# One order for eight sequences: steps of a two-layer transformer block merged anew, and a block buffer zeroed in eight pieces

## The chip, the cores and the metric

The kernel runs on one core of a Trainium2 chip. The metric is the device time of one execution in microseconds; the time of the kernel before is the median of three runs. The profile shows one execution of its own.

## The reference, cut to what matters

The input is eight sequences of 256 tokens by 128 channels, with a context of 256 by 64 for each. Four blocks follow one another, each added to x:

```python
x = x + _L0_xattn_ref(_layernorm(x), ctx, ...)   # 16 heads of 8: causal self and cross attention, then Wp
x = x + _L0_ffn_ref(_layernorm(x), ...)          # 8 experts, top 2 of a router, F = 512
x = x + _L1_xattn_ref(_layernorm(x), ctx, ctx, ...)  # one head of 128 against the context
x = x + _L1_ffn_ref(_layernorm(x), ...)
# the last one: 16 heads of 64 whose values are mixed per token out of 8 projections
mix_v = jnp.einsum('bthk,bthke->bthe', sigmoid(top2 of gate_v), one_hot)
v = jnp.einsum('bthe,bted->bhtd', mix_v, proj_v)
attn = softmax(q k^T) v
res = jnp.einsum('bthe,bthd,efd->bthf', mask_o, attn, Wo).sum(heads)
```

## The kernel before, in words

All of a sequence's tokens lie on the 128 partitions in two tiles. The work of a sequence is cut into small steps. A step is a name and a number, as ("a_score", 4), and each of the five engines has a function of that name if it has a part in the step. Three groups of steps make a sequence's A side: f (load, first norm, turning, and the eight projections f_stack 0 to 7 into stacked queries and keys), a (first attention: a_max finds row maxima, a_score makes scores and exponentials and, at some numbers, the products with the values; then a_heads, a_project, a_norm2, a_router and a_expert 0 to 7), and c (second attention: c_kv, c_norm, c_norm_apply, c_q, c_max, c_turn, c_out). The last block is the B side: b_norm, b_norm_apply, b_gates (gates, value projections), b_top2 0 to 2 (first maximum, second maximum, sigmoid and product), b_split 0 to 7 (queries and keys as high and low parts), b_max 0 to 7, b_shift, b_score 0 to 7, b_fill, b_mix 0 and 1, b_sel, b_attend 0 to 3, b_weigh, b_gather, b_out.

The A side uses PSUM banks 0 to 3 and the B side banks 4 to 7, so that the B side of a sequence can run within the A side of the next. An order written out by hand sets how. STEPS_A is the list of a sequence's A steps, where the f steps belong to the next sequence. STEPS_B is the list of its B steps, and AFTER_A gives for each of them behind which A step it comes (counted from the start of the same sequence; 56 steps make a sequence, so 65 is in the next one's A side). The last sequence has lists of its own, LAST_B and LAST_AFTER. The function merged() sorts all into one list, and every engine, SyncE's DMA queue too, goes through this one list and issues its own part of each step in that order. There is no other planning: between engines only semaphores order the work.

The mixing is done by matrix products with a block buffer, bd (128 x 2048 fp32). GpSimd zeroes it (line 1151 in b_gates, line 1156 after the second mixing), b_fill copies the mixing weights from DRAM onto its blocks with sixteen DMAs (line 466), b_mix multiplies (line 911), ScalarE copies the result to `at` (line 1106), SyncE stores it to v_d and loads it again, regrouped, as vb (lines 473 and 479), and b_attend multiplies with it (line 928). After the second zeroing b_sel (line 486) puts the output mask there, which b_gather uses (line 942). SyncE also carries f_load, which waits for the sequence's x_a before it loads the next x (line 431), the store and reload of the value projections (lines 443 and 450), and mix_d and sel_d (lines 457 and 458), which wait for the gate product of b_top2 2 (line 1433). The norms are applied by tensor_scalar in line 296, for the second attention in step c_norm_apply.

Of the kernel before, what the change touches and what calls it, by code (L numbers as in the profile page):

```python
# [35 lines left out]
def transformer_program(nc, a, out):  # L36
# [17 lines left out]
    with ctx:  # L54
# [91 lines left out]
        bd = sb("bd", [P, 2048])  # L146
# [17 lines left out]
        def dram(name, shape):  # L164
# [54 lines left out]
            b_mx=16, b_ct=1, b_cc=1, b_st=16, b_ex=16, b_mw=1, b_pd=16, b_pr=32, b_bz=2, b_md=32, b_dm=256, b_do=128,  # L219
# [131 lines left out]
        def run(name, first, end):  # L351
            return [(name, i) for i in range(first, end)]

        STEPS_A = [("a_values", 0), *run("a_max", 0, 7), ("a_shift", 0), ("a_score", 0), ("a_score", 1),
                   ("f_load", 0), *run("a_score", 2, 14), ("a_lastpv", 0), ("a_heads", 0), ("a_project", 0),
                   ("c_kv", 0), ("a_norm2", 0), ("a_norm2_apply", 0), ("a_router", 0), *run("a_expert", 0, 3),
                   ("f_norm", 0), *run("a_expert", 3, 8), ("f_norm_apply", 0), ("a_last", 0), ("c_norm", 0),
                   *run("f_stack", 0, 4), ("c_norm_apply", 0), ("c_q", 0), ("f_stack", 4), ("c_max", 0),
                   ("f_stack", 5), ("f_stack", 6), ("c_turn", 0), ("c_out", 0), ("f_stack", 7)]
        STEPS_B = [("b_norm", 0), ("b_norm_apply", 0), ("b_gates", 0), ("b_top2", 0),  # L360
                   ("b_split", 0), ("b_split", 1), ("b_top2", 1), *run("b_split", 2, 5), ("b_top2", 2),
                   *run("b_split", 5, 8), *run("b_max", 0, 8), ("b_shift", 0), ("b_score", 0), ("b_fill", 0),
                   ("b_mix", 0), ("b_mix", 1), ("b_score", 1), ("b_sel", 0), ("b_score", 2), ("b_score", 3),
                   ("b_attend", 0), ("b_score", 4), ("b_score", 5), ("b_attend", 1),
                   ("b_score", 6), ("b_score", 7), ("b_attend", 2), ("b_attend", 3), ("b_weigh", 0),
                   ("b_gather", 0), ("b_gather", 1), ("b_out", 0)]
        AFTER_A = (65, 69, 70, 71, 71, 72, 75, 75, 76, 77, 78, 79, 79, 81, 85, 86, 86, 90, 91, 91, 92, 92, 93, 96,
# [44 lines left out]
        def sequences(steps):  # L412
# [7 lines left out]
            with nc.Block(no_gpsimd_drain=True) as block:  # L420
# [704 lines left out]
                def _(pool):  # L1125
# [27 lines left out]
                    def b_mix(half):  # L1153
                        if half == 1:
                            pool.wait_ge(S["b_mm"], upto("b_mm", 2 * NT))
                            nc.gpsimd.memset(bd[:, :], 0.0).then_inc(S["b_bz"], 1)
# [336 lines left out]
```

## Time and profile before

| | |
|---|---|
| median of 3 runs | 1322.04 us (1322.01 to 1323.66) |
| profiled execution, its own time | 1322.67 us |
| its span | 1320.9 us |
| TensorE matmul busy | 1137.6 us, 86% |
| VectorE / ScalarE / GpSimd busy | 706.6 (53%) / 494.1 (37%) / 85.0 us (6%) |
| mean granted TensorE clock | 0.847 |

The span is the time from the first to the last instruction. A granted clock of 1.0 is 2.4 GHz and 0.5 is 1.2 GHz. Idle time of an engine is given with what ended it: "[2.10 <-DVE xn_a L296]" is an idle time of 2.10 us, ended by VectorE's instruction of line 296 that writes xn_a. PE is TensorE, DVE VectorE, ACT ScalarE, POOL GpSimd, SPq SyncE's DMA queue.

### The profile page before, as it was taken

How to read it: one execution, taken by the hardware profiler on the slowest of the kernel's cores; microseconds unless marked ns; L12 is line 12 of the kernel's file. 1: busy time of each engine (PE TensorE's matmuls, PEld its weight loads, DVE VectorE, ACT ScalarE, POOL GpSimd, SP SyncE). 2: the span in 40 equal slices, each digit the busy share in tenths (PEclk: the TensorE clock that was granted, in tenths of full speed). 3: DMA queues.
4: the chain of work that ended last, by engine and by line, in shares of the span. 5: the costliest groups of instructions: out<-in, count | busy, mean ns of one | idle time of the engine just before them, and what ended most of it. 6: DMA issues, size and time to landing. Idle time of an engine off the chain costs nothing.

```text
span 1320.9 us, 21222 instructions
## 1 busy us (share of the span) xinstructions
PE 1137.6 (86%) x8499; PEld 883.2 (67%) x8499; DVE 706.6 (53%) x1867; ACT 494.1 (37%) x1022; POOL 85.0 (6%) x134
## 2 busy tenths in 40 slices
PE   6888779989989988989988988988998998985696
PEld 4547545777668765877577855976577766874475
DVE  5514466646565557547665658546664656423500
ACT  4233415352534425451634334442535253422120
POOL 0010002000110002000200011000200011000000
PEclk8558959899789979998889978998889978977556
DMA  7000000242020420142022221042023210133222
GB/s 212 0 1 4 3 0 1 48 69 65 8 49 17 69 55 21 29 76 57 6 49 47 47 47 46 5 77 63 1 48 67 64 40 13 29 56 84 52 44 52
DMA packets 198032, 56.85 MB, mean 43 GB/s; under 512 B 173568, under 2 KB 193838, under 8 KB 197934
## 3 DMA queue, kind: packets, MB, share of 16 engines
q1 hardware_dynamic: 195630, 51.20, 19.9%
q10 hardware_dynamic: 2304, 4.29, 1.1%
q8 instruction: 67, 1.10, 0.3%
q14 instruction: 31, 0.25, 0.1%
HBM read 31.36 MB, written 24.12 MB: 42 GB/s over the span
## 4 chain that ended last, share of the span: by engine, by line
PE 75%; DVE 11%; ACT 7%; issue 3%; SPq 3%; DMA 2%; ACTq 0%; DVEq 0%
PE bank L928 10%; PE bank L737 10%; PE bank L773 9%; PE bank L884 5%; PE bank L663 5%; PE bank L843 4%; PE bank L624 3%; PE bank L678 3%; PE bank L588 3%; DVE negmax L1261 3%; ACT pa L1022 3%; PE bank L942 2%; PE bank L860 2%; PE bank L688 2%; PE bank L911 2%
## 5 line engine op out<-in xcount | busy, mean ns | idle before, releaser
L1022 ACT ACTIVATE pa<-bank 128x512 f32<-128x512 f32 x224 | 123.4, 596 | 122.8 <-PE bank L678 75.8
L1261 DVE TENSOR_REDUCE negmax<-bank 128x2 f32<-128x512 f32 (+1 forms) x224 | 139.0, 683 | 41.9 <-PE bank L526 22.1
L1039 ACT ACTIVATE pa<-bank,b_c 128x256 f32<-128x256 f32 x256 | 107.5, 471 | 128.6 <-PE bank L737 127.3
L928 PE MATMUL bank<-vb,pb 128*128 128x65 f32 x1024 | 137.1, 299 | 4.2 <-issue 4.2
L928 PEld LDWEIGHTS bank<-vb,pb 128*128 128x128 f32 x1024 | 132.8, 214 | 10.3 <-issue 7.9
L737 PE MATMUL bank<-xnT_a,w 128*128 128x256 f32 x512 | 138.1, 417 | 0.1
L773 PE MATMUL bank<-w,pa 128*128 128x128 f32 x1024 | 124.2, 276 | 0.0
L773 PEld LDWEIGHTS bank<-w,pa 128*128 128x128 f32 x1024 | 121.9, 192 | 3.2
L1101 ACT ACTIVATE pb<-bank 128x512 f32<-128x512 f32 x128 | 69.9, 602 | 125.4 <-PE bank L888 125.4
L737 PEld LDWEIGHTS bank<-xnT_a,w 128*128 128x128 f32 x512 | 101.1, 208 | 17.3 <-ACT pa L1039 0.5
L1415 DVE TENSOR_REDUCE negc<-bank 128x2 f32<-128x512 f32 x128 | 80.0, 684 | 58.8 <-PE bank L860 58.6
L1166 POOL TENSOR_SCALAR_AFFINE_SELECT pa<-pa 128x256 f32<-128x256 f32 (+1 forms) x96 | 53.8, 568 | 666.6 <-ACT pa L1022 665.4
L663 PE MATMUL bank<-pa,va 128*32 128x256 f32 (+1 forms) x1024 | 72.1, 412 | 6.6 <-issue 4.8
L1008 ACT ACTIVATE hi_part<-bank,lo_bias,lo_c 128x256 fp32r<-128x256 f32 x128 | 63.2, 568 | 32.5 <-PE bank L588 32.5
L843 PE MATMUL bank<-xnT_b,wqk_t 128*128 128x256 f32 x256 | 71.0, 409 | 4.5 <-DVE qk_lo L1407 4.5
L1111 ACT COPY pvs<-bank 128x512 f32<-128x512 f32 x16 | 16.8, 1049 | 151.1 <-PE bank L942 151.1
L624 PE MATMUL bank<-ks,qs 32*128 32x256 f32 x384 | 57.8, 407 | 13.8 <-DVE negmax L1261 10.7
L1251 DVE SCALAR_TENSOR_TENSOR qs<-bank,bias_c,hi_part 128x256 fp32r<-128x256 f32 x64 | 27.7, 480 | 77.1 <-ACT hi_part L1008 77.1
L678 PE MATMUL bank<-qs,ks 32*128 32x256 f32 x256 | 52.7, 392 | 18.1 <-ACT pa L1022 15.1
L588 PE MATMUL bank<-xnT_f,w_stack 128*128 128x256 f32 x192 | 56.0, 432 | 12.5 <-DVE qs L1251 9.6
L884 PE MATMUL bank<-qk_hi,qk_lo 64*128 64x256 f32 x256 | 55.5, 360 | 9.1 <-ACT pb L1101 7.8
L1346 DVE SCALAR_TENSOR_TENSOR x_a<-bank,wr,x_a 128x128 f32<-128x128 f32 x128 | 38.7, 343 | 44.4 <-PE bank L773 44.1
(240 smaller groups left out, 1706.3 us busy)
## 6 DMA issues: line engine op xcount, KB each, us to landing
v_d<-at SPq DMA_DIRECT2D x32, 256.0 KB, 3.3
vb<-v_d SPq DMA_DIRECT2D x32, 256.0 KB, 6.0
at_d<-at SPq DMA_DIRECT2D x32, 256.0 KB, 2.1
at<-at_d SPq DMA_DIRECT2D x32, 256.0 KB, 4.4
pv_d<-pvs SPq DMA_DIRECT2D x8, 512.0 KB, 3.1
pvs<-pv_d SPq DMA_DIRECT2D x16, 256.0 KB, 4.2
w<-in_L_ffn_W_dram ACTq DMA_DIRECT2D x1, 2048.0 KB, 11.5
bd<-mix_d SPq DMA_DIRECT2D x128, 8.0 KB
```

What stands on the lines that cost most here:

```text
L588: mm = pe.matmul(BA[2 + u % 2][:, c * T:(c + 1) * T], w_stack[0:rows, kind, g, :], rhs[:, :], start=True, stop=True)
L624: mm = pe.matmul(BA[j][:, c * T:(c + 1) * T], qs[strips[j], sc, g, qt * P:(qt + 1) * P], ks[strips[j], sc, g, :], start=(c == 0), stop=Tru ...
L663: mm = pe.matmul(dst, va[:, sc, kt, h * DV:h * DV + 32], rhs, start=(kt == 0), stop=(sc == SELF or kt == 1), skip_group_check=True)
L678: mm = pe.matmul(BA[i][:, kt * T:(kt + 1) * T], ks[strips[i], CROSS, k, kt * P:(kt + 1) * P], qs[strips[i], CROSS, k, :], start=True, stop ...
L737: mm = pe.matmul(BA[u % 2][:, c * T:(c + 1) * T], w1[:, e, f:f + P], xnT_a[:, :], start=True, stop=True)
L773: mm = pe.matmul(BA[2 + e % 2][:, t * P:(t + 1) * P], hT[:, (2 * e + f // 2) % 4, f % 2, t * P:(t + 1) * P], w2[:, e, f, :], start=(f == 0 ...
L843: mm = pe.matmul(BB[(u + 2) % 4][:, c * T:(c + 1) * T], wqk_t[:, u // 4, 2 * (u % 4) + c, :], xnT_b[:, :], start=True, stop=True)
L884: pe.matmul(BB[i][:, kt * T:(kt + 1) * T], kq[halves[i], 1, pr, keys], qq[halves[i], 0, pr, :], start=(kt == 0 and part == 0), stop=(part ...
L928: mm = pe.matmul(BB[2 + qt][:, i * (DH + 1):(i + 1) * (DH + 1)], pb[:, h % NPB, kt * T + qt * P:kt * T + (qt + 1) * P], vb[:, kt, h, :], s ...
L1022: nc.scalar.activation(pa[:, e % NPA, :], BA[e % 2][:, :], ACT.Exp, scale=SC0).then_inc(S["a_ex"], 1)
L1039: ins = nc.scalar.activation(hT[:, u % 4, c, :], BA[u % 2][:, c * T:(c + 1) * T], ACT.Relu, bias=b1_c[:, k:k + 1])
L1261: nc.vector.tensor_reduce(negmax[:, i:i + ng], BA[j][:, :].rearrange("p (g k) -> p g k", g=ng), AX, ALU.max, negate=True).then_inc(S["a_mx ...
```

## The change

Both lists of B steps, the list of A steps and their positions are written anew, and the memset of the block buffer is cut into eight of 256 columns each, with the semaphore counts that go with it. In the steady order the part around the second attention goes from "b_score 0, b_fill, b_mix 0, a_last, c_norm, f_stack 0 to 3, b_mix 1, c_norm_apply, b_score 1, c_q, f_stack 4, b_sel, c_max, b_score 2, f_stack 5 and 6, c_turn, b_score 3, b_attend 0, b_score 4, c_out, f_stack 7" to "b_fill, (f_norm_apply,) b_mix 0, a_last, c_norm, f_stack 0, b_score 0, b_mix 1, c_norm_apply, b_score 1, f_stack 1, c_q, f_stack 2, c_max, f_stack 3, b_sel, f_stack 4, c_turn, b_score 2, f_stack 5, c_out, f_stack 6, b_score 3, f_stack 7, b_attend 0, b_score 4".

```diff
-            b_mx=16, b_ct=1, b_cc=1, b_st=16, b_ex=16, b_mw=1, b_pd=16, b_pr=32, b_bz=2, b_md=32, b_dm=256, b_do=128,
+            b_mx=16, b_ct=1, b_cc=1, b_st=16, b_ex=16, b_mw=1, b_pd=16, b_pr=32, b_bz=16, b_md=32, b_dm=256, b_do=128,
...
-        STEPS_A = [("a_values", 0), *run("a_max", 0, 7), ("a_shift", 0), ("a_score", 0), ("a_score", 1),
-                   ("f_load", 0), *run("a_score", 2, 14), ("a_lastpv", 0), ("a_heads", 0), ("a_project", 0),
-                   ("c_kv", 0), ("a_norm2", 0), ("a_norm2_apply", 0), ("a_router", 0), *run("a_expert", 0, 3),
-                   ("f_norm", 0), *run("a_expert", 3, 8), ("f_norm_apply", 0), ("a_last", 0), ("c_norm", 0),
-                   *run("f_stack", 0, 4), ("c_norm_apply", 0), ("c_q", 0), ("f_stack", 4), ("c_max", 0),
-                   ("f_stack", 5), ("f_stack", 6), ("c_turn", 0), ("c_out", 0), ("f_stack", 7)]
-        STEPS_B = [("b_norm", 0), ("b_norm_apply", 0), ("b_gates", 0), ("b_top2", 0),
-                   ("b_split", 0), ("b_split", 1), ("b_top2", 1), *run("b_split", 2, 5), ("b_top2", 2),
-                   *run("b_split", 5, 8), *run("b_max", 0, 8), ("b_shift", 0), ("b_score", 0), ("b_fill", 0),
-                   ("b_mix", 0), ("b_mix", 1), ("b_score", 1), ("b_sel", 0), ("b_score", 2), ("b_score", 3),
-                   ("b_attend", 0), ("b_score", 4), ("b_score", 5), ("b_attend", 1),
-                   ("b_score", 6), ("b_score", 7), ("b_attend", 2), ("b_attend", 3), ("b_weigh", 0),
-                   ("b_gather", 0), ("b_gather", 1), ("b_out", 0)]
-        AFTER_A = (65, 69, 70, 71, 71, 72, 75, 75, 76, 77, 78, 79, 79, 81, 85, 86, 86, 90, 91, 91, 92, 92, 93, 96,
-                   96, 96, 102, 103, 105, 106, 109, 109, 109, 112, 113, 114, 114, 115, 116, 116, 119, 119, 120)
+        STEPS_A = [("a_values", 0), *run("a_max", 0, 7), ("a_shift", 0), *run("a_score", 0, 14), ("a_lastpv", 0),
+                   ("a_heads", 0), ("a_project", 0), ("a_norm2", 0), ("c_kv", 0), ("a_norm2_apply", 0),
+                   ("a_router", 0), ("a_expert", 0), ("a_expert", 1), ("f_load", 0), *run("a_expert", 2, 6),
+                   ("f_norm", 0), ("a_expert", 6), ("a_expert", 7), ("f_norm_apply", 0), ("a_last", 0),
+                   ("c_norm", 0), ("f_stack", 0), ("c_norm_apply", 0), ("f_stack", 1), ("c_q", 0), ("f_stack", 2),
+                   ("c_max", 0), ("f_stack", 3), ("f_stack", 4), ("c_turn", 0), ("f_stack", 5), ("c_out", 0),
+                   ("f_stack", 6), ("f_stack", 7)]
+        STEPS_B = [("b_norm", 0), ("b_norm_apply", 0), ("b_gates", 0), ("b_top2", 0), *run("b_split", 0, 8),
+                   *run("b_max", 0, 4), ("b_top2", 1), *run("b_max", 4, 8), ("b_top2", 2), ("b_shift", 0),
+                   ("b_fill", 0), ("b_mix", 0), ("b_score", 0), ("b_mix", 1), ("b_score", 1), ("b_sel", 0),
+                   ("b_score", 2), ("b_score", 3), ("b_attend", 0), ("b_score", 4), ("b_score", 5),
+                   ("b_attend", 1), ("b_score", 6), ("b_score", 7), ("b_attend", 2), ("b_attend", 3),
+                   ("b_weigh", 0), ("b_gather", 0), ("b_gather", 1), ("b_out", 0)]
+        AFTER_A = (67, 67, 68, 68, 70, 71, 74, 75, 76, 77, 78, 78, 79, 80, 84, 84, 85, 88, 88, 89, 89, 90, 93, 95,
+                   96, 99, 99, 100, 105, 107, 110, 111, 111, 112, 113, 114, 114, 115, 116, 116, 119, 119, 120)
...
-        LAST_B = [("b_norm", 0), ("b_norm_apply", 0), ("b_gates", 0), ("b_top2", 0), ("b_split", 0), ("b_top2", 1),
-                   *run("b_split", 1, 5), ("b_top2", 2), *run("b_split", 5, 8), ("b_max", 0), ("b_fill", 0),
-                   *run("b_max", 1, 4), ("b_mix", 0), ("b_sel", 0), ("b_mix", 1), *run("b_max", 4, 8),
+        LAST_B = [("b_norm", 0), ("b_norm_apply", 0), ("b_gates", 0), ("b_top2", 0), *run("b_split", 0, 3),
+                   ("b_top2", 1), ("b_top2", 2), *run("b_split", 3, 8), ("b_max", 0), ("b_fill", 0),
+                   *run("b_max", 1, 4), ("b_sel", 0), ("b_mix", 0), ("b_mix", 1), *run("b_max", 4, 8),
                    ("b_shift", 0), *run("b_score", 0, 4), ("b_attend", 0), ("b_score", 4), ("b_score", 5),
                    ("b_attend", 1), ("b_score", 6), ("b_score", 7), ("b_attend", 2), ("b_attend", 3),
-                   ("b_gather", 0), ("b_weigh", 0), ("b_gather", 1), ("b_out", 0)]
...
+                   ("b_gather", 0), ("b_gather", 1), ("b_weigh", 0), ("b_out", 0)]
...
                     def b_fill(_):
                         sp.wait_ge(S["b_md"], upto("b_md", 32))
-                        sp.wait_ge(S["b_bz"], upto("b_bz", 1))
+                        sp.wait_ge(S["b_bz"], upto("b_bz", 8))
...
                     def b_sel(_):
-                        sp.wait_ge(S["b_bz"], upto("b_bz", 2))
+                        sp.wait_ge(S["b_bz"], upto("b_bz", 16))
...
+                    def clear_blocks():
+                        for i in range(8):
+                            nc.gpsimd.memset(bd[:, 256 * i:256 * i + 256], 0.0).then_inc(S["b_bz"], 1)
+
                     def b_gates(_):
...
-                        nc.gpsimd.memset(bd[:, :], 0.0).then_inc(S["b_bz"], 1)
+                        clear_blocks()
 
                     def b_mix(half):
                         if half == 1:
                             pool.wait_ge(S["b_mm"], upto("b_mm", 2 * NT))
-                            nc.gpsimd.memset(bd[:, :], 0.0).then_inc(S["b_bz"], 1)
+                            clear_blocks()
```

## Rows read from the trace of the kernel before

**Rows 1.** The page: busy us, share and instructions of each engine; clock in tenths.

```profile
PE 1137.6 (86%) x8499; PEld 883.2 (67%) x8499; DVE 706.6 (53%) x1867; ACT 494.1 (37%) x1022; POOL 85.0 (6%) x134
PEclk8558959899789979998889978998889978977556
```

**Rows 2.** Stretches: length, busy us of each engine, granted clock, DMA share, GB/s.

```profile
559.81:705.78 145.97, 132.24 (x1058) 103.07 (x1057) 87.83 (x230) 60.64 (x126) 10.43 (x14) 0.91 0.22 43
...
576.00:582.00 6.00, 5.92 (x34) 4.58 (x36) 0.22 (x2) 2.96 (x6) 0.00 (x0) 0.72 1.17 190
...
628.00:642.00 14.00, 12.09 (x52) 6.48 (x48) 4.52 (x20) 6.39 (x12) 2.56 (x3) 0.63 0.05 14
...
563.00:593.00 30.00, 26.66 (x227) 21.88 (x226) 13.84 (x42) 17.05 (x37) 1.80 (x1) 0.94 0.51 84
```

**Rows 3.** Timeline of TensorE, second attention: start, length, instruction, idle before it.

```profile
570.05 1.99 PE L588 MATMUL bank<-xnT_f,w_stack 128*128 128x256 f32 x8 [1.24 <-DVE qs L1251]
...
576.08 0.44 PE L520 MATMUL bank<-ident,xn_a 128*128 128x128 f32 x2 [2.10 <-DVE xn_a L296]
```

**Rows 4.** Timeline of VectorE and GpSimd at the same place.

```profile
573.98 2.05 DVE L296 TENSOR_SCALAR xn_a<-x_a,mv_a,rstd_a 128x128 f32<-128x128 f32 x2
...
574.08 1.80 POOL L1156 MEMSET bd<- 128x2048 f32 x1 [58.09 <-PE bank L911]
```

**Rows 5.** Line 296: ns min/median/max, first and last start.

```profile
L296 DVE TENSOR_SCALAR xn_a<-x_a,mv_a,rstd_a x32: 339/346/1982, 106.1 to 1149.9; 128x128 f32<-128x128 f32 x32
```

**Rows 6.** Timeline of TensorE: score 3 of the first attention, and the second norm.

```profile
632.71 1.28 PE L678 MATMUL bank<-qs,ks 32*128 32x256 f32 x4 [0.48 <-ACT pa L1022]
...
672.45 0.69 PE L520 MATMUL bank<-ident,xn_a 128*128 128x128 f32 x2 [2.66 <-DVE xn_a L296]
```

**Rows 7.** Waits of TensorE in 559 to 705 us: total, times, longest; score 13.

```profile
PE bank L697 <- ACT pa L1022: 0.9, 2, 0.8
```

**Rows 8.** Line 1138: a memset of 256 columns on GpSimd, ns.

```profile
L1138 POOL MEMSET negc<- x1: 311/311/311, 2.6 to 2.6; 128x256 f32 x1
```

**Rows 9.** Timeline of VectorE, then of TensorE: top-2, reductions, products of experts.

```profile
650.62 0.68 DVE L312 TENSOR_REDUCE top_bm<-at 128x64 f32<-128x512 f32 x1
...
679.22 2.48 DVE L1415 TENSOR_REDUCE negc<-bank 128x2 f32<-128x512 f32 x4 [0.35 <-PE bank L860]
...
688.14 1.95 PE L773 MATMUL bank<-w,pa 128*128 128x128 f32 x16
...
705.71 3.84 PE L773 MATMUL bank<-w,pa 128*128 128x128 f32 x32
```

**Rows 10.** Timeline, last sequence: gate product, fills of the block buffer, first mixing.

```profile
1226.04 0.60 DVE L1433 TENSOR_TENSOR gates<-eg,top_b 128x256 f32<-128x256 f32 x1
...
1229.02 5.77 SPq L466 DMA_DIRECT2D bd<-mix_d  x16
...
1236.09 3.68 PE L911 MATMUL bank<-pvs,bd 64*128 64x64 f32 x32 [3.05 <-DMA bd<-mix_d]
```

**Rows 11.** Timeline of SyncE's queue in a steady period: mixing weights, fills.

```profile
674.12 0.66 SPq L457 DMA_DIRECT2D mix_d<-gates  x1
...
678.57 6.78 SPq L466 DMA_DIRECT2D bd<-mix_d  x16
```

**Rows 12.** Timeline of TensorE, first sequence, second attention.

```profile
149.25 0.44 PE L520 MATMUL bank<-ident,xn_a 128*128 128x128 f32 x2 [2.58 <-DVE xn_a L296]
```

**Rows 13.** Timeline of TensorE, last A window: mix 1, attend 0, C's output.

```profile
1150.40 2.00 PE L911 MATMUL bank<-pvs,bd 64*128 64x64 f32 x32 [1.14 <-ACT at L1106]
...
1164.60 7.06 PE L928 MATMUL bank<-vb,pb 128*128 128x65 f32 x32 [4.00 <-issue]
...
1173.60 2.07 PE L814 MATMUL bank<-pa 128*128 128x128 f32 x8
```

**Rows 14.** Timeline, last sequence: last value loads issued, attend 0.

```profile
1251.75 6.04 SPq L479 DMA_DIRECT2D vb<-v_d  x4
...
1264.11 7.09 PE L928 MATMUL bank<-vb,pb 128*128 128x65 f32 x32
```

More of the change, by code:

```diff
@@ L374, in transformer_program @@
                    ("b_shift", 0), *run("b_score", 0, 4), ("b_attend", 0), ("b_score", 4), ("b_score", 5),
                    ("b_attend", 1), ("b_score", 6), ("b_score", 7), ("b_attend", 2), ("b_attend", 3),
-                   ("b_gather", 0), ("b_weigh", 0), ("b_gather", 1), ("b_out", 0)]
-        LAST_AFTER = (57, 66, 75, 76, 76, 76, 76, 76, 76, 76, 76, 89, 104, 109, 109, 109, 109, 109, 110, 110, 110,
-                   110, 117, 117, 117, 117, 117, 117, 117, 117, 117, 117, 118, 126, 129, 136, 136, 143, 147, 149,
-                   149, 154, 154)
+                   ("b_gather", 0), ("b_gather", 1), ("b_weigh", 0), ("b_out", 0)]
@@ L380, in transformer_program @@
+        LAST_AFTER = (62, 66, 67, 70, 70, 73, 81, 86, 90, 90, 90, 90, 90, 90, 90, 90, 90, 90, 95, 111, 111, 112,
+                   113, 119, 121, 125, 129, 130, 130, 130, 130, 130, 130, 130, 130, 130, 135, 135, 135, 135, 135,
+                   135, 140)
         assert len(LAST_AFTER) == len(LAST_B)
```

## The prediction, made before the changed kernel ran

> **What bounds the kernel now.** I read the page's busy shares and its row of granted clock first. TensorE is busy for 86% of the span and no other engine for more than 53%, at a mean clock of 0.85 [rows 1]. So TensorE is the bound, and two things can be won: its idle time and the stretches in which it runs at half clock (1.2 instead of 2.4 GHz). Next come stretches of one steady period (sequence q on the A side, q-1 then q on the B side; 146 us). In it TensorE is busy for 132.2 of 146.0 us, at 0.91 [rows 2]. So a period holds 13.7 us of idle and 26 us at half clock (2 x 0.09 x 146), which cost 13 us more. Last I read TensorE's timeline through that period for where the idle lies, and those of VectorE and SyncE for what ends it.
>
> Three places hold most of it. (1) Around the start of the C attention TensorE waits 1.24 us for VectorE's splits, then 2.10 us for the normalised x [rows 3]. The second wait is not arithmetic: the pair of tensor_scalars took 2.05 us, and the 1.80 us clearing of the block buffer on GpSimd started 0.1 us after it [rows 4]; the median of one such operation is 0.346 us, so a free pair takes some 0.6 to 0.7 [rows 5]. Behind the two waits the clock is 0.72 for 6 us, 3.4 us at half, a loss of 1.7 us [rows 2]. (2) In the score stage single waits for ScalarE's exponentials of 0.5 to 0.8 us [rows 6, 7], with the clock at 0.63 over 14 us [rows 2]. (3) The second norm, 2.66 us waited for VectorE [rows 6].
>
> **The change, part by part.** Arithmetic and bytes are the same except for the clearing: one memset of 2048 columns becomes eight of 256. All the rest is order on each engine, also on SyncE's queue.
>
> *Region C of a steady period (six times, q = 1 to 6).* Before: score 0, mix 0, f_stack 0 to 3, mix 1, the normalised x, score 1. After: mix 0, f_stack 0, score 0, mix 1, normalised x, score 1, then f_stack 1 to 7 one by one between the steps of C. VectorE now has two splits instead of eight ahead of the normalised x, so it applies the norm while TensorE is at score 0 and mix 1: both waits have cover, and the clearing, which waits for mix 1, starts after the tensor_scalars. That returns 1.24 + 2.10 = 3.34 us [rows 3], and with no idle ahead of it the half-clock stretch should go, 1.7 us [rows 2]. Late next is ScalarE's order: the exponentials of C stand behind f_stack 2, and the turn of the probabilities waits for them. I put that at 0.7 us and other small ones at 0.6 (nearest rows: the waits of 0.48 [rows 6] and 1.24 [rows 3]); bounds 0 and 3.34, all of it coming back. Gain 3.34 + 1.7 - 1.3 = 3.7 us, times six: 22.4 us (bounds 10 and 30).
>
> *The clearing in pieces.* A piece of 256 columns took 0.31 us [rows 8], so eight take 1.80 to 2.5 us. At the start of a sequence's B side nobody waits; there its step also moves ahead of the masking of the fifth score step, but its wait has been met for long by then. If my order is off by a microsecond and a norm meets the clearing again, the rows give only the two ends: let in after one piece, 0.31 us [rows 8], or held through all eight, 1.8 us and more [rows 4]. Taken at nothing, with up to 1.9 us a period inside the bounds above.
> What bears on it is the Trainium skill, "SBUF — State Buffer", section "Who interferes with whom": VectorE in a two-port mode and GpSimd exclude each other for a whole instruction, whoever started first. By it the 2.05 us is that lock, pieces bring a meeting down to one piece, and the gain of region C stands even with the order slightly off; without it an unlucky meeting costs six times 1.7 us, 10 us of the sum.
>
> *The mixing and its feeders (SyncE, VectorE).* The second half of the top-2 (six operations of 512 columns, each like the first of [rows 9], 0.72 us apart, 4.3 us) and the gate product leave the score stage and go among the experts, the first ahead of the first accumulation, the second behind the third. f_load moves from early in the score stage to behind expert 1, so SyncE's queue no longer waits there for the projected x with the store and reload of the projected values behind it; these go out earlier. Nobody on TensorE waited for them: 0. The product, though, now comes late. From its end to the first mixing product the last sequence took 9.4 us (1226.64 to 1236.09) [rows 10]; in the period the stores and sixteen fills alone took 11.2 us [rows 11], some 12.5 with the landing (1.3 us in rows 10). Time available: expert 2's products end at 690.1, those of expert 7 at 709.5 [rows 9]; two B maxima steps fewer (by net count) lie between, and the tokens' turn is added, so 18.4 us. The product needs of that the reductions of two B maxima steps (2.48 us, behind 0.9 us of products), one accumulation of 0.6 and its own 2.7: 6.7. That leaves 11.7 us against 9.4 to 12.5: wait 0 to 0.8 us, taken at 0.3, inside the 0.6 above. Expert waits: VectorE has the router (twenty small operations, an estimated 0.2 us each) behind four reductions (2.5) and then the 4.3 us before the first accumulation, which comes at about 685 by this; it is needed by expert 2's products, which before started at 688.1 [rows 9]. Three us of cover, nothing charged.
>
> *Score stage and second norm (seven times).* B's norm and gates move one score step earlier or ahead: its turn fills the 0.48 us before score 3 [rows 6], and a split's products fill the 0.95 us (0.78 + 0.17) before score 13 [rows 7]. B maxima 0 and 1 go among the heads. Their reductions (four, 2.5 us) lie under TensorE's turns but push the heads' arithmetic by about 0.5 us, while the products fill what was waited. The 2.66 us before the router stays [rows 6]: its cover, the keys of C, is the same. Net 1.3 us, seven times: 9.1 us. Bounds: -0.4 us each (the reductions in full on the chain: 0.9 late against 0.5 filled) and +3.3 (half of the 5.2 us lost to half clock over 628 to 642 returns too).
>
> *First sequence without a B side.* Same interleave, and no mixing. 2.58 us were waited for the normalised x [rows 12], and the f_stacks that stood before it now fill the C chain. Gain 3 us (1 to 5).
>
> *Last A window.* The wait before mix 1 goes (1.14 us); B's attend 0 waited 4.00 us for values sent off behind mix 1 [rows 13]. These go 1.1 us earlier, and C's output products, 2.07 us at half clock and about 1.2 at full, move from behind it into its wait [rows 13]. Gain 3 us (1 to 5), counting 0.7 of clock.
>
> *Last sequence alone.* The gate product comes before splits 3 to 7 rather than before 5 to 7, some 1.0 us earlier; mix 0 waited for its fills [rows 10]. Against it, SyncE now stores the first mixed half behind the second clearing: two stores more ahead of the last loads, which were issued until 1257.8, while attend 0 began at 1264.1 [rows 14] with hardly any slack. Taken at +0.5 (-1 to +1.5). Exchanging b_weigh and b_gather 1 changes no engine's own order.
>
> Sum: 22.4 + 9.1 + 3 + 3 + 0.5 = 38 us. The profiled execution took 1322.7 us (span 1320.9), so 1284.7; the median of the runs lies 0.6 us below it: 1284.
>
> **Rivals.**
> - *Idle that only moves* (chance 0.25). ScalarE is busy for 17 of 30 us in region C [rows 2], in strict order, so f_stack's two activations may make C wait where it did not. For: TensorE waited for ScalarE at many places already [rows 6, 7]. Against: single waits there are under 1 us. Then region C gives 10 to 12 (no clock won), the score stage 4, the ends 4: 20 us, 1302.
> - *Clock comes back in the score stage too* (0.12). The half-clock stretch behind the B gathers ends once TensorE has been busy without a break; the gates' products now follow earlier. Two us more a sequence, 14 us: 1270. Against: the stretch before it (the A maxima, bound by VectorE's reductions) is unchanged.
> - *The fill comes late: slower* (0.07). The mixing waits for the fill, and everything on TensorE queues behind it. It outweighs the gain of 38 us over seven sequences from 5.4 us each, that is a stall of 3.7 plus 1.7 of clock: the way from product to last fill would have to take over 15.4 us, where rows show 9.4 to 12.5 [rows 10, 11]. At 17 us: 1330.
> - *No change* (0.04). The clearing still blocks a norm and the new order only exchanges waits: 1321.
>
> **How the numbers follow.** My forecast has 0.52, with a range of its own of 1276 to 1294. The range for 8 in 10 takes in the first rival and half of the second: 1267 to 1306. A measurement of this kernel tells 0.2% (2.6 us) from no change. Faster by more: 0.52 + 0.25 + 0.12 and a little of the rest, 0.90; within: 0.03; slower: 0.07.
>
> **What would show it.** Right: the tensor_scalar pair of C's norm at 0.6 us in every period; TensorE over 28 us or more of 30 busy in region C with its clock at 1.00; a period of about 141 us; half-clock time at the second norm unchanged. Wrong: waits of TensorE on the fills before mix 0 above 1 us; waits of the turn of C's probabilities above 1.5 us; an accumulation later than its expert's products. If the periods shrink by under 2 us each, the first rival holds.

## The result and the profile after

| | before | after |
|---|---|---|
| median | 1322.03 us (1318.88 to 1323.66) | 1278.06 us (1274.52 to 1278.99) |
| ratio, 95% interval | | 0.9666 (0.9645 to 0.9687) |
| profiled execution, its span | 1322.67, 1320.9 us | 1274.52, 1272.8 us |
| mean granted clock | 0.847 | 0.855 |

The kernel became 44 us faster, where 38 were forecast (1284, range 1267 to 1306). The page of the kernel after, to be read against [rows 1]: TensorE has 18.7 us less to do (the same 8499 products, more of them at full clock) in a span 48 us shorter.

```profile
PE 1118.9 (88%) x8499; PEld 874.8 (69%) x8499; DVE 700.1 (55%) x1867; ACT 491.0 (39%) x1022; POOL 82.8 (7%) x246
PEclk8557958899889979898889978998889988998556
```

The last products of expert 7 mark each sequence. In the chain that ended last (start, length, work) they stand like this after the change:

```profile
136.09 3.77 PE bank L773 x32
265.17 3.77 PE bank L773 x32
403.47 3.77 PE bank L773 x32
543.36 3.77 PE bank L773 x32
683.30 3.77 PE bank L773 x32
...
1103.14 3.77 PE bank L773 x32
```

From the second period on it is now 139.9 us each (the first is 138.3), where [rows 2] have one of 146.0; the kernel before alternated between 144.2 and some 146. Between the second and the last marker the kernel before took 1142.61 - 269.12 = 873.5 us, the one after 838.0: 35.5 us in six periods. Another 4.0 come ahead of the second marker, and 8.6 behind the last one (178.3 to 169.7 us). That makes 48.1 us between the two profiled spans; the medians give 44, since the profiled run of after was its fastest.

Windows of the kernel after (length, busy us of each engine, clock): the period of [rows 2], region C, the stretch behind the second norm, and the last A window.

```profile
543.36:683.30 139.94, 130.02 (x1057) 102.65 (x1057) 86.74 (x230) 60.13 (x126) 9.98 (x28) 0.91 0.23 45
547.00:577.00 30.00, 29.21 (x269) 24.51 (x266) 14.85 (x46) 19.45 (x42) 2.09 (x8) 1.00 0.52 84
650.00:660.00 10.00, 9.64 (x37) 7.91 (x38) 7.81 (x28) 3.66 (x10) 0.00 (x0) 0.58 0.00 0
...
1120.00:1140.00 20.00, 17.66 (x155) 15.46 (x154) 3.04 (x10) 6.51 (x12) 0.00 (x0) 0.93 0.35 51
```

TensorE's timeline of the same period (start, length, idle before): the two waits that remain in region C, then those of the heads and the second norm.

```profile
557.48 1.13 PE L799 MATMUL bank<-pa 128*128 128x256 f32 x4 [0.18 <-ACT pa L1067]
560.98 0.66 PE L806 MATMUL bank<-ident,pa 128*128 128x128 f32 x4 [0.52 <-ACT pa L1072]
...
645.01 0.44 PE L520 MATMUL bank<-ident,xn_a 128*128 128x128 f32 x2 [1.26 <-DVE xn_a L1306]
...
650.36 0.69 PE L520 MATMUL bank<-ident,xn_a 128*128 128x128 f32 x2 [2.67 <-DVE xn_a L296]
```

The reader is to see that the waits of [rows 3] are gone, that region C is busy for 29.21 of 30 us at full clock (26.66 at 0.94 before, [rows 2]), and that the second norm kept its wait (2.66 us in [rows 6]). Its half clock did not stay the same, it grew. Twelve us around that norm, before and then after, have a clock of 0.72 and 0.57, which is 6.7 and 10.3 us at half:

```profile
671.00:683.00 12.00, 10.55 (x51) 8.46 (x52) 8.12 (x31) 3.95 (x10) 0.00 (x0) 0.72 0.54 111
```

```profile
647.00:659.00 12.00, 9.33 (x35) 7.43 (x34) 9.43 (x41) 3.50 (x10) 0.00 (x0) 0.57 0.04 12
```

In the score stage it is the other way round. Fourteen us there, after the change, are at 0.76 in each of three periods; before it was 0.63 [rows 2] in the periods of some 146 us and 0.76 in those of 144.2:

```profile
606.00:620.00 14.00, 12.47 (x77) 7.35 (x73) 8.91 (x27) 6.81 (x14) 0.29 (x1) 0.76 0.05 17
```

Line 296, now never held up (against [rows 5]), and the clearing in pieces:

```profile
L296 DVE TENSOR_SCALAR xn_a<-x_a,mv_a,rstd_a x32: 337/343/348, 105.6 to 1110.4; 128x128 f32<-128x128 f32 x32
```

```profile
L1148 POOL MEMSET bd<- x128: 308/312/315, 92.8 to 1197.9; 128x256 f32 x128
```

The fill of the block buffer, which the prediction put at the edge, and the first mixing behind it, which did not wait (SyncE's queue, then TensorE):

```profile
675.20 0.37 SPq L457 DMA_DIRECT2D mix_d<-gates  x1
...
677.55 6.66 SPq L466 DMA_DIRECT2D bd<-mix_d  x16
```

```profile
687.43 2.00 PE L911 MATMUL bank<-pvs,bd 64*128 64x64 f32 x32
```

### The profile page after: what moved, and what is told of

Read it like the earlier page. It is cut to its first block, busy times and chain, and to the rows that moved or that the text cites. A ratio compares the mean times of both kernels' runs of the same rounds, so it can differ in the third digit from the quotient of the medians.

```text
span 1272.8 us, 21333 instructions
## 1 busy us (share of the span) xinstructions
PE 1118.9 (88%) x8499; PEld 874.8 (69%) x8499; DVE 700.1 (55%) x1867; ACT 491.0 (39%) x1022; POOL 82.8 (7%) x246
## 4 chain that ended last, share of the span: by engine, by line
PE 74%; DVE 12%; ACT 7%; issue 2%; SPq 2%; DMA 2%; ACTq 0%; DVEq 0%
PE bank L737 10%; PE bank L928 10%; PE bank L773 9%; PE bank L843 5%; PE bank L884 5%; PE bank L663 4%; PE bank L624 3%; PE bank L678 3%; DVE negmax L1265 3%; PE bank L911 3%; ACT pa L1022 2%; PE bank L588 2%; PE bank L942 2%; ACT hi_part L1008 2%; PE bank L832 2%
## 5 line engine op out<-in xcount | busy, mean ns | idle before, releaser
L737 PE MATMUL bank<-xnT_a,w 128*128 128x256 f32 x512 | 141.8, 429 | 0.1
L928 PEld LDWEIGHTS bank<-vb,pb 128*128 128x128 f32 x1024 | 129.6, 209 | 7.8 <-ACT pb L1101 3.0
L928 PE MATMUL bank<-vb,pb 128*128 128x65 f32 x1024 | 133.8, 294 | 1.2 <-ACT pb L1101 0.8
L737 PEld LDWEIGHTS bank<-xnT_a,w 128*128 128x128 f32 x512 | 107.0, 219 | 18.4 <-ACT pa L1039 0.7
L1148 POOL MEMSET bd<- 128x256 f32 x128 | 33.4, 312 | 745.2 <-PE bank L911 414.3
L1411 DVE TENSOR_TENSOR qk_lo<-bank,qk_hi 128x512 fp32r<-128x512 f32 x64 | 43.8, 690 | 65.9 <-ACT qk_hi L1093 65.9
L1111 ACT COPY pvs<-bank 128x512 f32<-128x512 f32 x16 | 16.9, 1058 | 150.3 <-PE bank L942 150.2
L1170 POOL TENSOR_SCALAR_AFFINE_SELECT pa<-pa 128x256 f32<-128x256 f32 (+1 forms) x96 | 46.7, 495 | 369.5 <-ACT pa L1022 368.3
L663 PE MATMUL bank<-pa,va 128*32 128x256 f32 (+1 forms) x1024 | 66.1, 385 | 4.4 <-issue 2.5
L884 PE MATMUL bank<-qk_hi,qk_lo 64*128 64x256 f32 x256 | 57.1, 356 | 9.9 <-ACT pb L1101 8.5
L678 PE MATMUL bank<-qs,ks 32*128 32x256 f32 x256 | 52.3, 393 | 14.8 <-ACT pa L1022 11.7
L843 PEld LDWEIGHTS bank<-xnT_b,wqk_t 128*128 128x128 f32 x256 | 44.9, 191 | 23.4 <-DVE qk_lo L1411 13.1
## 6 DMA issues: line engine op xcount, KB each, us to landing
w<-in_L_ffn_W_dram ACTq DMA_DIRECT2D x1, 2048.0 KB, 10.5
```

Source lines behind the costliest of these rows:

```text
L663: mm = pe.matmul(dst, va[:, sc, kt, h * DV:h * DV + 32], rhs, start=(kt == 0), stop=(sc == SELF or kt == 1), skip_group_check=True)
L678: mm = pe.matmul(BA[i][:, kt * T:(kt + 1) * T], ks[strips[i], CROSS, k, kt * P:(kt + 1) * P], qs[strips[i], CROSS, k, :], start=True, stop ...
L737: mm = pe.matmul(BA[u % 2][:, c * T:(c + 1) * T], w1[:, e, f:f + P], xnT_a[:, :], start=True, stop=True)
L843: mm = pe.matmul(BB[(u + 2) % 4][:, c * T:(c + 1) * T], wqk_t[:, u // 4, 2 * (u % 4) + c, :], xnT_b[:, :], start=True, stop=True)
L884: pe.matmul(BB[i][:, kt * T:(kt + 1) * T], kq[halves[i], 1, pr, keys], qq[halves[i], 0, pr, :], start=(kt == 0 and part == 0), stop=(part ...
L928: mm = pe.matmul(BB[2 + qt][:, i * (DH + 1):(i + 1) * (DH + 1)], pb[:, h % NPB, kt * T + qt * P:kt * T + (qt + 1) * P], vb[:, kt, h, :], s ...
```

## The experiments

The median of the kernel before in the same group of runs is given with the first of each group. Four groups: the first four below, the next four, then e4, e12 and e11, and last e14.

**1. The new order with one whole clearing (e1).**

```diff
-                        for i in range(8):
-                            nc.gpsimd.memset(bd[:, 256 * i:256 * i + 256], 0.0).then_inc(S["b_bz"], 1)
+                        for i in range(1):
+                            nc.gpsimd.memset(bd[:, :], 0.0).then_inc(S["b_bz"], 8)
```

> The changed kernel with the block buffer zeroed in one memset of 2048 columns again; the new order stays. Theory (the order is what counts, since the norm of C is now applied before the clearing starts): no change within 2 us of the changed kernel, about 1278 us, and the tensor_scalar pair of C's norm stays at 0.6 to 0.7 us. Rival (the pieces count): the pair or another VectorE operation meets the 1.80 us clearing in each of six periods and the time rises by 6 to 10 us, to 1285 to 1288.

Measured: 1277.75 us (before 1320.10), ratio 0.9681 (0.9654 to 0.9707). With the new order the pieces bring nothing: the clearing no longer meets a norm (line 296 is 348 ns at the longest).

**2. The old order with the clearing in pieces (e2).** The diff's `clear_blocks`, `b_bz=16` and the two waits, without the lists.

> The kernel before with nothing changed but the clearing in eight pieces. Theory A (one VectorE instruction is let in after one piece): the pair of tensor_scalars falls from 2.05 us to 0.9 to 1.2, TensorE's wait before C's turn from 2.10 to about 1.1, some 6 us over six periods and up to 10 more if the half-clock stretch behind it goes: 1306 to 1316 us. Theory B (the pieces follow one another so closely that VectorE is held through all eight, 2.1 us): 1322 to 1324 us.

Measured: 1405.27 us, ratio 1.0679 (1.0601 to 1.0757), and a miss for both theories. The four runs spread from 1388.25 to 1418.56 us, more than those of any other kernel here, so it is 68 to 98 us slower (85 by the median); the profile is of the fastest. Line 296 in this kernel, then TensorE's timeline, SyncE's queue and the window behind:

```profile
L296 DVE TENSOR_SCALAR xn_a<-x_a,mv_a,rstd_a x32: 336/343/492, 104.5 to 1219.5; 128x128 f32<-128x128 f32 x32
```

```profile
598.87 0.44 PE L520 MATMUL bank<-ident,xn_a 128*128 128x128 f32 x2 [0.65 <-DVE xn_a L296]
...
610.51 5.99 PE L928 MATMUL bank<-vb,pb 128*128 128x65 f32 x32 [2.40 <-ACT pb L1101]
```

```profile
599.89 5.74 SPq L479 DMA_DIRECT2D vb<-v_d  x4
```

```profile
611.00:669.00 58.00, 57.07 (x343) 47.71 (x342) 24.11 (x50) 6.99 (x12) 0.00 (x0) 0.51 0.17 38
```

The pieces did their work: the longest tensor_scalar fell from 1982 ns [rows 5] to 492, and the norm's wait from 2.10 us [rows 3] to 0.65. But the mixed values, which SyncE stores and loads again, came no earlier behind mix 1. From mix 1's first product TensorE now needed 11.9 us to be ready for attend 0 and not 14.5 (1.45 of it from the norm's wait, the rest from products that ran at full clock), and it waited there for 2.40. The wait is put down to ScalarE's exponentials, which is the last event the profile shows; that it is the reload is suggested by the distance from the reload's first issue to attend 0, and shown by experiment 5. It is 610.51 - 599.89 = 10.6 us here, with a wait. In the kernel before, these two stood like this:

```profile
575.65 5.94 SPq L479 DMA_DIRECT2D vb<-v_d  x4
```

```profile
586.51 3.79 PE L928 MATMUL bank<-vb,pb 128*128 128x65 f32 x32
```

10.9 us, no wait. Over e2's six periods the distance with a wait is 10.5 to 11.4 us, and the kernel before has one period with a wait of 0.19 us at 11.2: it had a few tenths of a microsecond to spare at this place, at most. Behind the 2.40 us TensorE ran at half clock for 58 us although busy for 57.1 of them. From marker to marker the periods alternate between 164.4 and 149.6 us; in the shorter ones, with waits of 2.3 to 3.2 us, the clock is back after some 10 us. Why the same wait costs so differently stays open.

**3. The new kernel with region C in its old order (e3).** The A list, the places of b_score 0, b_fill, b_mix and the positions of region C as before; score stage, top-2, gates and pieces as after.

> The changed kernel with the second attention's region in its old order (f_stack 0 to 3 together, score 0 ahead of mix 0, mix 1 behind f_stack 3, C's output behind attend 0 and score 4); experts, score stage, last sequence and the pieces stay new. Theory (most of the gain is region C, with its half-clock stretch, and the last A window): the time rises by 22 to 32 us, to 1300 to 1310. Rival (score stage and tail made most of it): it rises by less than 12, to 1290 at most.

Measured: 1338.39 us, ratio 1.0135 (1.0105 to 1.0165): not 10 to 20 us of gain but 18 of loss. It has the pieces and the old order of region C like e2. Its trace is of the longest of the four runs (1359.65 us; the others took 1336.77 to 1339.16), so it tells where the kernel waits, and not how the 18 us divide. Attend 0 waits in each of the six periods, for 2.3 to 3.1 us, for instance

```profile
593.41 6.85 PE L927 MATMUL bank<-vb,pb 128*128 128x65 f32 x31 [2.56 <-ACT pb L1100]
```

at 10.8 us behind the first issue of its reload. So e2's wait is in this kernel too; that it makes up the 18 us isn't shown.

**4. The kernel before with region C alone in its new order (e5).** The inverse, with the whole clearing:

```diff
-                   *run("f_stack", 0, 4), ("c_norm_apply", 0), ("c_q", 0), ("f_stack", 4), ("c_max", 0),
-                   ("f_stack", 5), ("f_stack", 6), ("c_turn", 0), ("c_out", 0), ("f_stack", 7)]
+                   ("f_stack", 0), ("c_norm_apply", 0), ("f_stack", 1), ("c_q", 0), ("f_stack", 2),
+                   ("c_max", 0), ("f_stack", 3), ("f_stack", 4), ("c_turn", 0), ("f_stack", 5), ("c_out", 0),
+                   ("f_stack", 6), ("f_stack", 7)]
...
-                   *run("b_split", 5, 8), *run("b_max", 0, 8), ("b_shift", 0), ("b_score", 0), ("b_fill", 0),
-                   ("b_mix", 0), ("b_mix", 1), ("b_score", 1), ("b_sel", 0), ("b_score", 2), ("b_score", 3),
+                   *run("b_split", 5, 8), *run("b_max", 0, 8), ("b_shift", 0), ("b_fill", 0), ("b_mix", 0),
+                   ("b_score", 0), ("b_mix", 1), ("b_score", 1), ("b_sel", 0), ("b_score", 2), ("b_score", 3),
```

> The complement: the kernel before with nothing new but region C's order (mix 0, f_stack 0, score 0, mix 1, C's norm, the other f_stacks one by one, C's output ahead of attend 0). The clearing is one memset. Theory: six periods give 3.5 to 4 us each, the first sequence 3, the last A window 5 to 6: 30 us, about 1292. Rival (the parts only work together): at most 15 us, 1307 or more.

Measured: 1291.11 us, ratio 0.9782 (0.9757 to 0.9807): 29.0 us of gain, as the theory had it (30). The prediction's terms that lie in this part are region C, first sequence and last A window: 22.4 + 3 + 3 = 28.4 us. The parts don't add up, though: region C alone gives -29, everything else alone +18 (e3), both together -44.

**5. The pieces in the old order, mix 1 earlier (e9).** e2 with mix 1 and its store behind f_stack 0 instead of f_stack 3: the position 102 becomes 99.

> The kernel before with the clearing in eight pieces and, of the new order, only one move: mix 1 behind f_stack 0 instead of behind f_stack 3. Theory (with the pieces alone TensorE reached attend 0 before the regrouped values had landed, waited 2.4 us and more there, and then ran at half clock for 8 to 45 us; mix 1 some 3 to 4 us earlier takes that away): 1295 to 1312 us, faster than the kernel before, and no wait of attend 0 on the values above 1 us in the steady periods. Rival (the pieces themselves upset something else, on GpSimd or VectorE): it stays above 1370.

Measured: 1330.65 us (before 1324.26), ratio 1.0057 (1.0037 to 1.0076). Its timeline of TensorE:

```profile
580.34 0.44 PE L520 MATMUL bank<-ident,xn_a 128*128 128x128 f32 x2 [2.54 <-DVE xn_a L296]
...
590.77 3.79 PE L928 MATMUL bank<-vb,pb 128*128 128x65 f32 x32
```

One number in a list takes nearly all of e2's loss away, and in the steady periods attend 0 no longer waits: the wait for the regrouped values, with the half clock behind it, is e2's cause. The forecast of 1295 to 1312 was still missed. Without f_stack 1 to 3 ahead of mix 1 the clearing is early, yet the norm waits 2.54 us again while line 296 itself takes 348 ns at most. So that wait belongs to the order too, not only to the clearing. VectorE has all the splits of f_stack 0 to 3 ahead of the norm, and the last of them waits for ScalarE:

```profile
578.89 0.88 DVE L1255 SCALAR_TENSOR_TENSOR ks<-bank,bias_c,hi_part 128x256 fp32r<-128x256 f32 x2 [1.37 <-ACT hi_part L1008]
579.68 0.60 DVE L296 TENSOR_SCALAR xn_a<-x_a,mv_a,rstd_a 128x128 f32<-128x128 f32 x2
```

**6. The new kernel with the mixing later (e10).** Mix 1 moves from behind f_stack 0 to behind c_max, and so behind score 1, f_stack 1 and f_stack 2 (position 99 to 104); score 1 keeps its place. Of the edit:

```diff
-                    ("b_fill", 0), ("b_mix", 0), ("b_score", 0), ("b_mix", 1), ("b_score", 1), ("b_sel", 0),
+                    ("b_fill", 0), ("b_mix", 0), ("b_score", 0), ("b_score", 1), ("b_mix", 1), ("b_sel", 0),
```

> The changed kernel with mix 1 moved back, behind score 1 and f_stack 2 (7 to 8 us later), so that its store and reload end some 4 to 5 us after TensorE reaches attend 0. Theory: a wait of 4 to 5 us before attend 0 in each of six periods and a half-clock stretch behind each: 30 us of waits and 20 to 90 us of clock, 1325 to 1400 us. Rival (f_stacks one by one and the norm's place are the gain, the mixing's lead is not needed): at most 12 us over the changed kernel, 1290.

Measured: 1363.10 us, ratio 1.0304 (1.0285 to 1.0324): the place of mix 1 alone decides between 44 us of gain and 39 of loss. All waits of line 928 in this kernel (total, times, longest):

```profile
PE bank L928 <- issue: 35.0, 8, 8.1
```

Its period is 150.2 us, 10.3 longer than after. In the one read (from 565.8), 4.5 of that are this wait and 1.5 a wait for C's norm, for which mix 1 had been cover; TensorE is busy for 134.8 us instead of 130.0 with the same 1057 products, which is clock.

**7. The gate product behind expert 5 instead of expert 3 (e6).** One position, 90 to 92.

> The changed kernel with the gate product (b_top2 2) behind expert 5's accumulation instead of expert 3's, about 7 us later. In the changed kernel the last fill was issued at 684.2 and mix 0 began at 687.4, so some 2 us of slack. Theory: mix 0 waits about 5 us for its fills in each of seven periods, 35 us, and the clock may fall to half behind each wait, 10 to 60 us more: 1315 to 1370 us. Rival (there is much more slack than I think, or the DMAs go faster without neighbours): under 1290.

Measured: 1304.78 us, ratio 0.9855 (0.983 to 0.9881), 27 us slower than after. The first mixing now waits for its fills:

```profile
PE bank L911 <- DMA bd<-mix_d: 18.7, 7, 3.6
```

That is 2.7 us on average, not the 5 of the theory, and the time lies between its 1315 and the rival's 1290. The prediction's rival "fill late" is a real mechanism. Two experts later makes a wait of up to 3.6 us; the kernel after, with the product where the change puts it, has no such wait.

**8. The last sequence kept busy (e8).** Products on constants that nobody reads, in the last sequence alone (22 before split 7; more before maxima, scores and mixing):

```diff
+                    def warm(n):
+                        if now[0] == B - 1:
+                            for _ in range(n):
+                                pe.matmul(BA[3][:, 0:T], w1[:, 0, 0:P], w1[:, 0, 0:T], start=True, stop=True)
```

> The changed kernel with extra products of constants on TensorE (128x256, into a free bank, read by nobody) ahead of its waits in the last sequence: 22 before split 7, 5, 3 and 2 around the maxima, 6 and 4 before the two mixings, 6 before the shift, 2 before each score that waits. In the changed kernel the last 85 us ran at half clock though TensorE was 93% busy in most of them. Theory (the clock stays low because of the short idle times; filling them brings it back): the tail's products take half the time, 15 to 28 us less, 1250 to 1263. Rival (the extra products only take time): 1278 to 1290.

Measured: 1266.65 us, ratio 0.9572 (0.9552 to 0.9592), 11 us faster than after; the theory had 1250 to 1263. In the kernel after, then in this one, the last stretches are

```profile
1180.00:1205.00 25.00, 14.75 (x107) 12.01 (x108) 10.87 (x18) 2.73 (x5) 2.09 (x8) 0.50 0.20 25
1205.00:1272.80 67.80, 52.00 (x332) 46.13 (x330) 5.34 (x18) 10.75 (x18) 0.00 (x0) 0.55 0.28 59
```

```profile
1180.00:1205.00 25.00, 25.00 (x174) 19.84 (x173) 10.22 (x17) 2.74 (x5) 2.09 (x8) 1.00 0.13 11
1205.00:1263.00 58.00, 43.28 (x371) 37.55 (x369) 6.13 (x20) 10.76 (x18) 0.00 (x0) 0.82 0.36 76
```

**9. C's output products late in the last A window (e4).** Behind score 4 of sequence 6, as before the change, in this window only.

```diff
+            order.remove(("c_out", 0, B - 1))
+            order.insert(order.index(("b_score", 4, B - 2)) + 1, ("c_out", 0, B - 1))
```

> The changed kernel with one step moved back in the last A window only: C's output (c_out of sequence 7) behind attend 0 and score 4 of sequence 6, as in the kernel before. Theory (c_out's products shorten the wait before attend 0, and a longer wait there brings half clock behind it, which made the last window give 6.7 us instead of the 3 I had forecast): 3 to 7 us slower than the changed kernel, 1281 to 1285 us, with a wait of 2 to 3 us before attend 0 and half clock behind it. Rival (the earlier mixing alone did it): within 1.5 us.

Measured: 1284.63 us (before 1323.26), ratio 0.9715 (0.9685 to 0.9746), against 0.9666 for after: 6.5 us, as the theory had it, but not by the wait of 2 to 3 us that it expected. Attend 0 waited 0.94 us; the price is in the clock:

```profile
1120.00:1140.00 20.00, 16.54 (x95) 14.38 (x96) 2.92 (x9) 4.86 (x11) 0.00 (x0) 0.58 0.57 72
```

The kernel after has 0.93 there. In both the clock falls ahead of attend 0, behind waits of 0.89 and 1.84 us in C's chain. With C's output of 2.07 us in the gap before attend 0 it came back within 3.4 us, without it after 17.

**10. Five constant products before the second norm's turn (e12).** `warm(5, BA[0])` in a_norm2_apply, every sequence.

> The changed kernel with five extra products of constants (128x256, into a bank free at that point, read by nobody) in the 2.67 us that TensorE waits for the second norm, in all eight sequences. Behind that wait the clock was 0.58 over 10 us, 8.4 us at half. Theory: the half-clock stretch goes, up to 4 us a sequence, 15 to 32 us in all: 1246 to 1263 us. Rival (other waits around it, 1.26 and 0.46 us, keep the clock low all the same): 1275 to 1281.

Measured: 1287.61 us, ratio 0.9743 (0.9708 to 0.9777): 9.5 us slower than after, a miss. Its windows: the norm's stretch, and a later one.

```profile
650.00:660.00 10.00, 8.25 (x53) 6.71 (x52) 8.25 (x31) 3.72 (x10) 0.00 (x0) 1.00 0.00 1
578.00:603.00 25.00, 24.74 (x150) 19.73 (x152) 13.82 (x27) 0.14 (x1) 0.00 (x0) 0.50 0.29 64
```

Behind the norm the clock is full where it was 0.58, and most periods took 138 us. But in one (145.3 us) a stretch at half clock, with TensorE busy for 24.7 of 25 us, came up among B's scores, though the gap ahead of it (0.69 us) is the same as in the others. And the part behind the last marker is 18 us longer, more than the periods had won. Of it 17 lie in the last A window, and there a gap did change:

```profile
1117.85 5.03 PE L938 MATMUL bank<-vb,pb 128*128 128x65 f32 x32 [2.45 <-issue]
```

```profile
1120.00:1171.00 51.00, 40.59 (x263) 37.23 (x262) 7.10 (x31) 6.42 (x10) 2.08 (x8) 0.50 0.18 42
```

With full clock ahead of it TensorE was ready for attend 0 12.1 us after mix 1's first product, and 13.6 in the kernel after; the values were no earlier, so it waited 2.45 us instead of 0.75, and the next 51 us ran at half clock. It is e2's sequence of events again: time won ahead of attend 0 is waited for there.

**11. All gaps filled (e11).** The norm's five, one product before scores 1 and 2 and before the waits of maxima 5 and 6, about half of e8's fillers in the last sequence, and there b_sel behind mix 1 instead of ahead of mix 0.

```diff
+                     def warm(n, bank, width=T):
+                         for _ in range(n):
+                             pe.matmul(bank[:, 0:width], w_stack[:, Q0, 0, :], w_stack[:, Q0, 0:width // P, :],
+                                       start=True, stop=True)
...
+                                if m >= 5 and c == 0 and now[0] > 0:
+                                    warm(1, BB[0], P)
...
+                                    if n in (1, 2) and kt == 0 and i == 0:
+                                        warm(1, BA[3])
...
+                        warm(5, BA[0])
```

> As the kernel with the norm's gap filled, and besides one product more before scores 1 and 2, one of 128 columns before each wait of the last two rounds of the first attention's maxima, and the waits of the last sequence filled with fewer products than in the earlier trial (12 before split 7 instead of 22, 1 to 3 elsewhere instead of 2 to 6), its b_sel behind mix 1. Theory: 4 us a sequence at the norm, 2 to 5 at maxima and scores, and 15 to 20 in the last sequence: 1205 to 1240 us. Rival (the extra products delay what they stand before as much as the clock gives back): 1262 or more.

Measured: 1239.40 us, ratio 0.9395 (0.9339 to 0.945): 6% faster than before and 39 us faster than the changed kernel, with 300 products more. What b_sel's move gives of that wasn't measured alone. Its page, and four of its markers:

```profile
PE 1133.6 (91%) x8799; PEld 884.9 (71%) x8799; DVE 699.2 (56%) x1867; ACT 489.0 (39%) x1022; POOL 83.0 (7%) x246
PEclk8559857999899998999899999999899999965997
```

```profile
404.04 3.77 PE bank L787 x32
540.80 3.77 PE bank L787 x32
677.52 3.77 PE bank L787 x32
814.44 3.77 PE bank L787 x32
```

**12. The same without the norm's filler (e14).**

```diff
-                        warm(5, BA[0])
```

> The kernel with every gap filled (1239.4 us), without its five constant products ahead of the second norm's turn; the fillers before scores 1 and 2, before the waits of A maxima 5 and 6 and in the last sequence stay. Their result is read by nobody. Theory: the norm's filler alone only moved the half clock to the scores (1287.6 us against 1278.1), so it is worth nothing without the others but something with them: the norm's wait of 2.67 us and the half clock behind it come back in each of seven periods, about 2 to 3 us each, and the kernel takes 1255 to 1262 us, with a period of 139 us. Rival: the norm's filler costs as much as it gives here too (its products hold up what stands behind them), the gain of the filled kernel comes from the fillers before the scores and maxima, and this kernel takes 1230 to 1240 us.

Measured: 1253.22 us (before 1324.49), ratio 0.9475 (0.9447 to 0.9503); periods of 137.2 to 139.9 us; the theory had 1255 to 1262. So the norm's filler is worth 14 us by the medians and 11 by the ratios beside the others (e11's slowest run, 1251.73 us, lies among e14's), and costs 9.5 without them. Fillers can't be priced one by one here.

## Why the prediction was right, step by step

- *Region C* (22.4 us, with first sequence and last window 28.4): right in place and mechanism. Both waits of [rows 3] went; late next was ScalarE, as said, with 0.18 and 0.52 us where 1.3 were allowed. Idle returned 3.34 - 0.70 = 2.6 us; the clock went from 0.94 to 1.00 over 30 us, 1.8 us (1.7 forecast). 4.4 us a period instead of 3.7; from the marker to the first wait among the next sequence's maxima the traces have 54.7 and 50.4 us. Alone it gave 29 us (e5).
- *Idle that only moves*: this rival fell, since the periods shrank by 5.9 us on average, not under 2. In the old order such a move did happen (e2), to attend 0 and not, as the rival had it, to ScalarE.
- *Clearing in pieces at nothing*: right for the new order (e1). The step held it to be an insurance worth up to 1.9 us a period. In the old order it costs 68 to 98 us (e2). The Trainium skill ("SBUF — State Buffer", "Who interferes with whom") has the lock for a whole instruction; the trace agrees: 1982 ns beside a whole clearing, 492 beside pieces, a delay of 149 ns, under the 312 of one piece. That was right and still decided nothing, since a second wait stood right behind the first.
- *What the prediction did not see*: the lead of the mixing. It named attend 0's wait only for the last window. In the steady period attend 0 was covered by a few tenths of a microsecond, so any waiting taken away between mix 1 and attend 0 had to come back there. The new order gave both at once: mix 1 moved ahead of f_stack 1 to 3, so f_stack 1 to 7 and C's output stand between it and attend 0, where f_stack 4 to 6 stood, and 16.1 us pass from one to the other instead of 14.5. e10 shows that the gain hangs on this. The working had no term for it, so that no loss came from it was luck.
- *Mixing and feeders*: nobody waited, as charged (0.3 us were allowed). The fills' issues end at 684.2, with the landing of 1.3 us [rows 10] at 685.5, so 1.9 us are to spare, where the working had -0.8 to 2.3 (11.7 against 12.5 and 9.4); e6 confirms the rival's mechanism at a distance of two experts.
- *Score stage and second norm* (1.3 us a sequence): 5.9 - 4.4 = 1.5 a period on average, which is right in the waits and lucky in the size. The waits of [rows 7] and the 0.48 of [rows 6] are gone, the wait at the heads grew from 0.83 to 1.26 us (the push by VectorE's reductions, put at 0.5), and the norm's is unchanged, all as forecast. The clock is not. The prediction had the half-clock time at the second norm unchanged, and it grew by 3.6 us in the period read, a loss of 1.8. Where the period before was some 146 us the score stage gave that much back (0.63 to 0.76 over 14 us: 3.6 us less at half), and where it was 144.2 it had nothing to give. So against the short periods the whole change is worth 4.3 us, region C's part alone, and against the long ones 6 us and more. *Clock comes back in the score stage too* therefore came true in the long periods only and was lost again at the norm: the period's mean clock stays at 0.91. Why the norm's half-clock stretch grew isn't shown.
- *First sequence*: 3 + 1.3 forecast ahead of the second marker, 4.0 measured.
- *The mis-sized term* is the last A window, 3 us. From the marker to attend 1 it returned 6.5 us (34.9 to 28.4): attend 0 waited 0.75 instead of 4.00 us and took 3.76 instead of 7.06 [rows 13]. I had counted 0.7 us of clock; e4 gives 6.5 for C's output in the gap alone.
- *Last sequence alone*: 0.5 forecast, 8.6 - 6.5 = 2.1 us measured. Of these, 1.8 come ahead of the last B norm, mostly from the output products of sequence 6 at full clock instead of half (line 953: 2.06 us instead of 3.57). Another 0.75 come up to mix 0: its wait of 3.05 us for the fills [rows 10] became one of 1.69 for a reduction, while the wait before split 7 grew from 3.81 to 5.81. Against these, 0.44 are lost up to attend 0, which now waits 0.40.

Sum of what was measured between the two profiled spans: 4.0 + 35.5 + 8.6 against 4.3 + 30 + 3.5.

## What to carry to other kernels

Before a wait is taken away, measure how far its successors are from waiting: the distance from a transfer's issue to its first reader, in a place where it waits and in one where it doesn't, bounds the slack (here 10.9 without a wait against 10.5 to 11.4 with one). A gain upstream is kept only when the slowest chain downstream (here mix, store, reload, attend) starts earlier by as much. And price a gap by what the clock does behind it: in e2 gaps of much the same length stood in periods of 149.6 and of 164.4 us. A filler must be judged on the whole run.

## What the runs showed of the hardware that was not expected

- Half clock can stay although TensorE is busy. In e2 it was busy for 57.1 of 58 us at a granted clock of 0.51, and in e12 for 24.7 of 25 at 0.50. In both kernels other periods with the same order ran at full clock in the same place. What decides between the two isn't settled.
- The same four stores of the mixed values occupied SyncE's queue for 8.07 us in the kernel before, 4.92 after and 12.09 in e10, because ScalarE's copies that they wait for are spread over that time (the two pairs stand 7.1, 3.9 and 11.1 us apart). Their length is no transfer time.
- 300 useless products made the kernel 39 us faster; TensorE's busy time rose by 14.7 us, and the mean clock of the profiled run (e11's slowest) from 0.855 to 0.912.
